# Graph network layer: own products in the second node stage added on TensorE and VectorE, turned

## What is computed

```python
def _rgcn_edge_conv(h, xe, src, dst, etype, w, rt, b):
    m = jax.nn.relu(h[src] + xe)
    n = h.shape[0]
    seg = etype * n + dst
    sums = jax.ops.segment_sum(m, seg, num_segments=R * n)
    cnt = jax.ops.segment_sum(jnp.ones((m.shape[0],), m.dtype), seg, num_segments=R * n)
    mean = sums / jnp.maximum(cnt, 1.0)[:, None]
    hr = mean.reshape(R, n, -1)
    out = jnp.einsum('rnd,rdo->no', hr, w)
    out = out + h @ rt + b
    return out
...
for l in range(L):
    h = _rgcn_edge_conv(h, xe, src, dst, edge_type, weight[l], root[l], bias[l])
    h = _batch_norm(h, bn_gamma[l], bn_beta[l])
    if l != L - 1:
        h = jax.nn.relu(h)
```

## Time and profile before

| | us |
|---|---|
| median of 3 runs (2580.36 to 2582.49) | 2582.11 |
| the profiled execution | 2575.32 |
| its span | 2573.5 |
| second node stage, first load of sums issued to last turning done | 2281.89 to 2437.2 |

### The profile page before, as it was taken

One profiled execution on the slowest core, in us unless ns is written; L12 is line 12 of the kernel. 1 busy time (PEld: TensorE's weight loads), 2 busy tenths in 40 slices (PEclk: granted clock), 3 DMA queues, 4 the chain that ended last, 5 costly groups with the idle time before them and its releaser, 6 DMA issues. The chain is left out here.

```text
span 2573.5 us, 51149 instructions
## 1 busy us (share of the span) xinstructions
PE 2254.8 (88%) x19360; PEld 2198.6 (85%) x19360; DVE 1924.6 (75%) x5073; ACT 1021.9 (40%) x2126; POOL 1642.8 (64%) x1612
## 2 busy tenths in 40 slices
PE   2499999999998889899799999899989999967866
PEld 1399999899898888899799999899989999966845
DVE  8699998898897778488878767676767667735654
ACT  0255565545555544344223222222222222234655
POOL 7677777777777777300477777777777777754100
PEclk7699999999999999999899999999999999989976
DMA  8844555454454444499522332323232323356799
GB/s 336 315 155 136 173 170 166 153 180 158 162 165 154 137 133 144 176 418 417 200 84 75 101 101 76 99 76 101 76 100 77 101 76 96 94 180 232 256 385 404
DMA packets 242709, 439.86 MB, mean 171 GB/s; under 512 B 39171, under 2 KB 144222, under 8 KB 242460
## 3 DMA queue, kind: packets, MB, share of 16 engines
q1 hardware_dynamic: 169878, 251.58, 27.8%
q0 software_dynamic: 50496, 103.39, 13.4%
q10 hardware_dynamic: 22086, 81.56, 7.9%
HBM read 256.98 MB, written 179.40 MB: 170 GB/s over the span
## 5 line engine op out<-in xcount | busy, mean ns | idle before, releaser
L1469 PE MATMUL ps_y<-arena 128*128 128x128 f32 x11032 | 1396.0, 279 | 64.3 <-DVE arena L1073 64.0
L1469 PEld LDWEIGHTS ps_y<-arena 128*128 128x128 f32 x11032 | 1327.3, 196 | 71.0 <-DVE arena L1073 71.0
L769 POOL DMA_INDIRECT acc<-arena x788 | 785.1, 996 | 258.0 <-issue 230.6
L1073 DVE SCALAR_TENSOR_TENSOR arena<-ps_s,arena 128x512 f32<-128x512 f32 (+1 forms) x1386 | 842.7, 679 | 22.5 <-PE ps_y L1470 18.4
L758 POOL DMA_INDIRECT arena<-h_rows,arena x394 | 397.8, 1010 | 299.8 <-DMA h_rows<-chunk_mem 180.0
L758 POOL DMA_INDIRECT arena<-in_x_dram,arena x394 | 403.1, 1023 | 126.6 <-issue 118.9
L1259 ACT ACTIVATE arena<-ps_y 128x512 f32<-128x512 f32 (+1 forms) x198 | 117.0, 591 | 533.5 <-PE ps_y L1470 533.4
L1470 PE MATMUL ps_y<-arena 128*128 128x128 f32 x1576 | 308.3, 278 | 0.0
L1251 ACT ACTIVATE arena<-ps_t 128x512 f32<-128x512 f32 (+1 forms) x198 | 116.6, 589 | 339.4 <-PE ps_t L1444 336.9
L1059 DVE TENSOR_TENSOR arena<-arena,bn_b 128x512 f32<-128x512 f32 (+1 forms) x99 | 69.1, 698 | 241.4 <-DMA arena<-h_rows,arena 241.2
L1470 PEld LDWEIGHTS ps_y<-arena 128*128 128x128 f32 x1576 | 243.2, 195 | 0.0
(11 more groups left out here) (199 smaller groups left out, 2305.6 us busy)
## 6 DMA issues: line engine op xcount, KB each, us to landing
arena<-in_edge_attr_dram SPq DMA_DIRECT2D x190, 256.0 KB
chunk_mem<-acc SPq DMA_DIRECT2D x55, 512.0 KB, 12.5
acc<-arena ACTq DMA_DIRECT2D x28, 896.0 KB, 22.1
acc<-arena SPq DMA_DIRECT2D x28, 896.0 KB
arena<-in_x_dram SPq DMA_DIRECT2D x45, 512.0 KB, 9.9
arena<-acc SPq DMA_DIRECT2D x43, 512.0 KB, 11.3
chunk_mem<-hn_rows SPq DMA_DIRECT2D x41, 512.0 KB, 11.7
out_dram<-arena ACTq DMA_DIRECT2D x38, 512.0 KB, 8.9
```

The costliest lines, as they stand in the source:

```text
L769: pool.indirect_dma_start(out=acc[l], out_offset=at(idx_t[:, t:t + 1]), in_=ob[:, gg % OB, t // NG, :], in_offset=None, **how).then_inc(sc ...
L1073: ins = v.scalar_tensor_tensor(mk[:, m, r, 0:n], ps_type[gg % 2][:, 0:n], float(r), mt[:, gg % MT, 0:n], ALU.is_equal, ALU.mult)
L1469: te.matmul(ps_y[gg % 2][:, c], mk[:, gg % MKS[l], r, c], w_sb[l][:, r * D:(r + 1) * D], start=r == 0, stop=False)
```

## The change

`OWN_FIRST` has chunk 1 in place of 2. The first product is made turned, with the root as weights, in one matmul of 512 columns. GpSimd's adds are gone. In the second node stage the sums of chunk c are turned, as they are loaded, into one of three bank pairs (`ps_s`, `ps_y`, `ps_o` by c % 3). For a chunk in `ROWS[1]` TensorE adds the own product into the same banks (`product_added`) and ScalarE copies the result out. For a held chunk VectorE adds the turned product from `own_at(i)` and writes the kept place (`add_held`), in place of ScalarE's copy. TensorE's order is sums and product of c - 2, then rows of c. SyncE issues the rows of c + 2 behind the sums of c.

```diff
-    OWN_FIRST = sorted([*range(0, 37, 2), 27, 31, 37])
+    OWN_FIRST = sorted([0, 1, *range(4, 37, 2), 27, 31, 37])
...
+        STOOD = {2: 1, 11: 6, 13: 10, 33: 30, 35: 34}
...
+        def sum_banks(c):
+            return (ps_s, ps_y, ps_o)[c % 3]
...
-                        sp.wait_ge(held_added, OWN_FIRST.index((18, 20, 22, 24)[k - XLATE]) + 1)
+                        sp.wait_ge(held_added, owns_done((18, 20, 22, 24)[k - XLATE]))
...
-                    if l == 1 and c in ROWS[1] and ROWS[1].index(c) + AHEAD + 1 in range(SLOTS, NR[1]):
-                        node_rows(ROWS[1].index(c) + AHEAD + 1)
...
                         table_dma(sp, acc_at(1, c), acc[1], c, y_in(c), True)
+                        if c + AHEAD in ROWS[1][SLOTS:]:
+                            node_rows(ROWS[1].index(c + AHEAD))
...
-            for i, c in enumerate(OWN_FIRST):
-                pool.wait_ge(first_ready, 2 * i + 2)
-                pool.wait_ge(y_in(c), y_count(c))
-                rows = acc_at(1, c).rearrange("p c d -> p (c d)")
-                gp.tensor_tensor(rows, rows, own_at(i), ALU.add).then_inc(held_added, 1)
...
+                def add_held(c):
+                    i = OWN_FIRST.index(c)
+                    dve.wait_ge(first_ready, 2 * i + 2)
+                    dve.wait_ge(sT_ps, NC + c + 1)
+                    for q in range(2):
+                        cols_ = slice(q * W4, (q + 1) * W4)
+                        v.tensor_tensor(sums_at(c)[:, cols_], sum_banks(c)[q][:, :], own_at(i)[:, cols_], ALU.add).then_inc(held_added, 1)
...
-                    for c in range(NC + 2):
-                        if c - 1 in ROWS[1]:
-                            add_own(c - 1)
-                        if c >= 2:
-                            features(c - 2)
+                    for c in range(NC + 1):
+                        if c in OWN_FIRST:
+                            add_held(c)
+                        if c >= 1:
+                            features(c - 1)
...
                 def keep_sums(c):
+                    u = turned_count(1, c) - 1
+                    if c in STOOD:
+                        act.wait_ge(held_added, owns_done(STOOD[c]))
                     for q in range(2):
-                        act.wait_ge(sT_ps, NC + c + 1)
+                        act.wait_ge(own_ps, 2 * u + q + 1)
...
-                        if c >= 2:
+                        if c - 2 in ROWS[1]:
                             keep_sums(c - 2)
...
-                for j in range(H):
-                    last = te.matmul(ps_t[1][:, j * D:(j + 1) * D], ht[:, k % 2, j * D:(j + 1) * D], root_sb[:, D:2 * D],
-                                     start=True, stop=True)
-                last.then_inc(first_ps, 1)
+                te.matmul(ps_t[1][:, :], root_sb[:, D:2 * D], ht[:, k % 2, 0:W4], start=True, stop=True).then_inc(first_ps, 1)
...
+                        pe.wait_ge(y_in(c), y_count(c))
+                        if c == 0:
+                            pe.wait_ge(stat_read, 2 * NC)
+                        elif c == 1:
+                            pe.wait_ge(join_ready, 2)
+                        elif c - 3 in OWN_FIRST:
+                            pe.wait_ge(held_added, owns_done(c - 3))
+                        elif c >= 3:
+                            pe.wait_ge(keep_ready, keeps_done(c - 3))
+                    to = ps_s if l == 0 else sum_banks(c)
+                    alone = l == 0 or c in OWN_FIRST
+                    for j in range(CW):
+                        last = te.matmul(to[j // H][:, (j % H) * D:(j % H + 1) * D], acc_at(l, c)[:, j, :], ident[:, :],
+                                         is_transpose=True, start=alone or j % H == 0, stop=alone)
+                    last.then_inc(sT_ps, 1)
+
+                def product_added(c):
+                    u = turned_count(1, c) - 1
                     for q in range(2):
                         pe.wait_ge(hT_ready, 2 * u + q + 1)
                         for j in range(H):
                             k = (q * H + j) * D
+                            last = te.matmul(sum_banks(c)[q][:, j * D:(j + 1) * D], root_sb[:, D:2 * D], ht[:, u % 2, k:k + D],
+                                             start=False, stop=j == H - 1)
                         last.then_inc(own_ps, 1)
```

More of the change, by code:

```diff
@@ L401, in gnn_kernel, with own_banks, owns_done, keeps_done @@
         ps_turn, ps_type = ps_t[0], ps_s
-        def own_banks(l, c):
-            return (ps_o, ps_y)[(c if l == 0 else ROWS[1].index(c)) % 2]
+        def own_banks(c):
+            return (ps_o, ps_y)[c % 2]
+        def sum_banks(c):
+            return (ps_s, ps_y, ps_o)[c % 3]
+        def owns_done(c):
+            return 2 * sum(1 for k in OWN_FIRST if k <= c)
+        def keeps_done(c):
+            return 2 * sum(1 for k in ROWS[1] if k <= c)
         pool_own = sem("pool_own")
@@ L710, in _ @@
                         elif YLATE <= c < YLATE + SLOTS:
[L711 removed]
+                            sp.wait_ge(held_added, owns_done((4, 12, 14, 16)[c - YLATE]))
                         elif c >= YLATE + SLOTS:
@@ L1548, in sums_turned @@
                 def sums_turned(c, l=l):
-                    if l == 1 and c in OWN_FIRST:
-                        pe.wait_ge(held_added, OWN_FIRST.index(c) + 1)
-                    else:
-                        pe.wait_ge(sum_ready, 2 * turned_count(l, c))
                     if l == 0:
+                        pe.wait_ge(sum_ready, 2 * c + 2)
                         wait(pe, stat_read, 2 * c)
                     else:
-                        pe.wait_ge(stat_read, 2 * NC)
-                        wait(pe, keep_ready, 2 * c)
+                        pe.wait_ge(y_in(c), y_count(c))
@@ L1558, in sums_turned @@
                     for j in range(CW):
-                        last = te.transpose(ps_s[j // H][:, (j % H) * D:(j % H + 1) * D], acc_at(l, c)[:, j, :], ident[:, :])
+                        last = te.matmul(to[j // H][:, (j % H) * D:(j % H + 1) * D], acc_at(l, c)[:, j, :], ident[:, :],
+                                         is_transpose=True, start=alone or j % H == 0, stop=alone)
                     last.then_inc(sT_ps, 1)
-                behind = 2
-                for c in range(NC + behind):
-                    if c < NC and (l == 0 or c not in OWN_FIRST):
-                        rows_turned(c)
-                    if 0 <= c - 1 < NC and (l == 0 or c - 1 not in OWN_FIRST):
-                        own_product(c - 1)
-                    if c >= behind:
-                        sums_turned(c - behind)
+                def product_added(c):
+                    u = turned_count(1, c) - 1
+                    for q in range(2):
+                        pe.wait_ge(hT_ready, 2 * u + q + 1)
+                        for j in range(H):
+                            k = (q * H + j) * D
+                            last = te.matmul(sum_banks(c)[q][:, j * D:(j + 1) * D], root_sb[:, D:2 * D], ht[:, u % 2, k:k + D],
+                                             start=False, stop=j == H - 1)
+                        last.then_inc(own_ps, 1)
@@ new lines, in _ @@
+                if l == 0:
+                    for c in range(NC + 2):
+                        if c < NC:
+                            rows_turned(c)
+                        if 0 <= c - 1 < NC:
+                            own_product(c - 1)
+                        if c >= 2:
+                            sums_turned(c - 2)
+                else:
+                    for c in range(NC + 2):
+                        if c >= 2:
+                            sums_turned(c - 2)
+                        if c - 2 in ROWS[1]:
+                            product_added(c - 2)
+                        if c in ROWS[1]:
+                            rows_turned(c)
```

34 lines of the change are left out of this document (16 added, 18 removed).

## The result

The changed kernel's median is 2545.99 us (2544.63 to 2547.97, 4 runs) beside 2581.24 for the kernel before on the same chip (2579.32 to 2582.49). The ratio is 0.9865 with a 95% interval of 0.9848 to 0.9882. The profiled execution took 2544.63 us, its span 2542.8; before, 2573.5. Forecast were a median of 2551.6 and a profiled execution of 2544.8.

A forecast was written before the change was run, and what follows sets the result against it. TensorE was taken to bound the stage: work 114.4 us plus 3.0 half clock, 2.5 VectorE and 1.0 loads, from 2285.8 to 2406.7 instead of 2437.2. That is 30.5 us less, a median of 2551.6 us, range 2543 to 2570.

The forecast's parts named there:

- half clock at the start: Second node stage's start: TensorE runs 6 us at half speed as now, 3.0 us lost.
- (1): Second node stage: GpSimd's 22 adds go, removing 2.35 us at the start and the whole 8.9 us loop.
- the rounds: 2336 to 2364: four loops of SyncE issue, load and GpSimd add, some 8.9 us for two chunks each.
- (2): VectorE loses 54 adds, gains 44 from PSUM at 1.27 us a pair, bound 1.51; sum 91 us, below 114.4.
- (3): ScalarE loses 22 pairs of copies of 1.09 us, keeps 69 us and is nowhere last.
- (4): TensorE's counts stay; 8 turnings into a bank left open take 0.87 us, bounds 0.87 or 1.79.
- The rival that had them cost as products: Turnings of sums take 1.79 us for 8 instead of 0.87, 45 us more: 2597; slower had chance 0.05.
- (5): Three bank pairs remove 0.6 us a pair of chunks; VectorE delays the run of held chunks about 2.5 us.
- (6): SyncE issues rows(c + 2) behind sums(c), later than before; load waits put at 1 us.
- the rival in which loads set the pace: Loads needing 9.9 us make four chunks take 11.2, stage 14.6 us more: 2566; chance 0.14 to 2572.
- (7): Second edge loop: first product in two instructions instead of eight; nothing taken, at most 2 us of gain.
- (8): Behind the stage: last product after last turning, x loads start earlier before TensorE's end; nothing lost.

The follow-up runs named there:

- e2: The kernel before with only SyncE's new order, rows of c + 2 behind the sums of c: stage 147.2 us, ratio 0.9944 to the kernel before.
- e13: The kernel before with only SyncE's new order, repeated on another chip: stage 142.2 us, ratio 0.9961 to the kernel before.
- e5: The kernel before with each of GpSimd's adds on 8 of 1024 columns: stage 143.9 us, ratio 0.995 to the kernel before.
- e1: The changed kernel with SyncE's old order, rows issued ahead of the sums: stage 169.6 us, ratio 0.9964 to the kernel before.
- e6: The changed kernel run again, unaltered: median 2540.42 us, stage 126.9 us, ratio 0.9866 to the kernel before.
- e10: The changed kernel with the second layer's statistics taken of one tile in place of four: stage 125.7 us, ratio 0.9872 to the kernel before.
- e3: The changed kernel with two bank pairs in turn instead of three: stage 150.8 us, ratio 0.9919 to the kernel before.
- e8: The changed kernel with each first product as four matmuls of 128 columns instead of one of 512: median 2540.55 us, ratio 0.9869 to the kernel before.
- e7: The kernel before run again, unaltered, for its trace: stage 156.3 us; the kernel before took 2573.83 us on that chip.
- e12: The changed kernel with SyncE's old order, repeated on another chip: stage 169.9 us, ratio 0.9998 to the kernel before.
- e9: The changed kernel with 150 turnings of the identity put on TensorE ahead of the stage: median 2539.16 us, stage 124.8 us, ratio 0.986.

## Where the prediction was right and where it was not

**The sum.** Forecast: TensorE from 2285.8 to 2406.7, 120.9 us. Measured: 2285.65 to 2406.6, 120.95. It is made up otherwise:

| | forecast | measured |
|---|---|---|
| work at full clock | 114.4 | 114.4, by the same 0.87 and 1.79 |
| half clock at the start | 3.0 | 3.2 (four steps in 6.70 instead of 3.49) |
| VectorE in the run of held chunks | 2.5 | 0 |
| waits for loads | 1.0 | 1.5 (0.5 + 0.2 + 0.8) |
| wait for ScalarE | 0 | 0.8 |
| starting again behind waits | 0 | 1.0 (the rest; the four steps that follow a wait take some 0.2 more than 0.87 each) |

**(1) GpSimd's adds:** right. The first turning came with the landing, and the rounds are gone. But I gave all of the rounds to the adds and took the new order for a part that costs or gives about 1 us. e2, e13 and e5 show that either would have ended or shortened them, and e1 that the adds' new place without the new order would have been worse than before. The step gave the right number because both were in the change, which is luck as far as the order goes.

**(2) VectorE's adds:** 1.29 us a pair and 1.27 where they run on; taken 1.27, bound 1.51. The timeline of VectorE (start, us, engine, line, what, in brackets the wait ahead) in the new kernel:

```profile
2308.33 1.29 DVE L1159 TENSOR_TENSOR arena<-ps_o,arena 128x512 f32<-128x512 f32 x2 [0.74 <-PE ps_o L1576]
```

**(3) ScalarE:** its copies were as cheap as said, but "nowhere last" was wrong once, for 0.76 us. The timelines of ScalarE and TensorE in the new kernel:

```profile
2365.13 1.09 ACT L1362 ACTIVATE arena<-ps_o 128x512 f32<-128x512 f32 x2 [1.18 <-DVE arena L1159]
2366.81 1.45 ACT L1337 ACTIVATE ht<-ps_t,bn_col 128x512 f32<-128x512 f32 x2 [0.59 <-PE ps_t L1546]
2368.40 1.06 PE L1546 MATMUL ps_t<-ident,chunk_mem 128*128 128x128 f32 x8 [0.76 <-ACT ht L1337]
```

The last turning is that of the rows of chunk 39. It wants the banks `ps_t` back from ScalarE's scaling of the rows of 38 (1.45 us), and between the two turnings of rows TensorE has only the sums of 37, a held chunk (0.87 us). So the wait lies in TensorE's new order wherever rows follow rows with one held chunk's sums between them; in e6 and e10 the same wait appears at the start too, for chunk 3, where in this trace the half clock hid it. It is not VectorE's doing, though the first line looks like it. There `keep_sums` of chunk 35 stands 1.18 us for VectorE's add of 34, which frees the place it writes (`STOOD`, in the diff). But ScalarE was then idle for 0.59 us more before the rows of 38 were turned, so that stand reached nobody; and e10, where VectorE has slack, has the 0.8 us all the same:

```profile
PE ps_t L1547 <- ACT ht L1338: 1.6, 3, 0.8
```

**(4) Turnings into an open bank:** 0.87 us for 8, the lower bound, in all pairs. The rival that had them cost as products, the one on the slower side, needed 1.79 and did not occur.

**(5) Three bank pairs:** 4.41 us for a pair of chunks, for a forecast of 4.40. e3 adds that two bank pairs would not have been enough, by 24 us. The 2.5 us for VectorE in the run of held chunks were the term that failed. VectorE was full there, as the walk said, and did not come to the point of holding TensorE: two laps of loads held TensorE by 1.5 us in the same stretch, and with that the slack of the banks sufficed. This reading of why is argued; that TensorE did not wait for VectorE is shown, by the waits, and e10 bounds what VectorE can cost at under 1 us. e3, where VectorE is on the chain with two pairs, speaks for the slack of the third.

**(6) SyncE and the loads:** 1.0 us forecast, 1.5 measured. Rows landed in 7.0 us where the earlier trace rows had 4.2, and the two loads of the laps took 6.11 and 6.04 us, where 5.4 was the median for such places; sums into the first places took what they had before (5.9, and 6.0 in the trace of before). More was moved at a time: 373 GB/s in 2344 to 2366, for 221 in 2336 to 2368 before. The DMA issues of the new kernel's stage (count, KB, median us to landing):

```profile
arena<-acc SPq DMA_DIRECT2D x19, 512.0 KB, 5.9
chunk_mem<-h_rows SPq DMA_DIRECT2D x15, 512.0 KB, 7.0
```

The laps at 2344 are 7.1 and 7.2 us for four chunks, not the 11.2 of the rival in which loads set the pace. That rival was the nearest to come true: at 6.1 us TensorE waits under 1 us a lap, and I would expect each further microsecond of landing to be one of the stage in each lap, which no run shows.

**(7) The first product:** nothing, within 0.5 us of the median, where e8 could test it. The last scatter of the edge loop began at 2275.90, before at 2276.19. On slower chips it may be worth more; the prediction had a bound of 2 us, and an edge loop 12 to 19 us shorter there, if it comes from this, is outside it.

**(8) Behind the stage:** nothing lost, 136.2 us for 136.3. The last stage's first turning came 6.2 us behind TensorE's last step, before 6.7.

**The median** came 5.6 us under the forecast though the profiled execution was right to 0.2. I took the gain from one profiled execution and set it against a median, and a single execution lies some us off its kernel's median: 5.9 and 1.4 under it in the comparison above, but 5.2 over it for the new kernel in e6 and 2.5 over for the one before in e7. So the 0.2 is finer than one execution can tell and in part luck. The gain of the medians, 35.2 and 33.4 us, is 3 to 5 more than the 30.5 of the sum; the runs don't say where that lies.

## What to carry to other kernels

Before moving an add to another engine, look at what its completion is counted for: here the DMA queue's head waited for it, and the same move makes the stage 43 us longer or leaves it at TensorE's pace, depending on what stands at that head. A product accumulated in the bank of a turning saves another engine's pass but prolongs the bank's stay by the product and the copy, so count bank pairs by that stay and not by the number of steps. An engine that a window shows full is a suspect only; the view of waits of the bounding engine, or half of its work taken away, says whether it costs anything.

## What the runs showed of the hardware

- **Turnings left open.** 8 f32 turnings take 0.87 us and the product into the same bank 1.79, the same as with closed banks, in some 27 pairs.
- **Load bandwidth.** In five windows on end, 2372 to 2392, the new kernel moved 410 to 420 GB/s with DMA shares of 1.02 to 1.04, while TensorE was busy for 4.00 of 4 us in each. The Trainium skill, "DMA: Bandwidth & Descriptors", gives some 358 GB/s in its opening table as the limit of a core at HBM, and in its section "Bandwidth" says that this is a core's share when both cores of a pair stream. The program here runs on one core, and the windows lie 15 to 17% above that figure (they count spills to device memory with the loads), so it is no limit in this case.
- **Chips.** The same kernel before took 2574, 2581, 3009 and 3051 us in four comparisons, on three chips at least. The single steps of the stage are alike on all; what differs is the edge loops, 1034 us against 1221 to 1259 for the second, with gaps on TensorE of up to 2.6 us that the view puts down to issue, hundreds of them. Their cause is open.
- **The clock behind short waits.** In e12 TensorE is idle for 6.4 us in the round shown, and the next 5.3 us of its work run at a granted clock of 0.52 (the 1.2 GHz level is 0.50). In e9, after TensorE had been kept busy from 2267.72 on, it was 0.57 in 2268 to 2272 and 1.00 in all windows that follow, the landing included.
